# Attention probabilities of a Perceiver layer: half of each head transposed by DMA and DVE block transposes instead of TensorE

## The reference

```python
q = (query @ w_q).reshape(B, Q, HEADS, HEAD_DIM).transpose(0, 2, 1, 3)
k = (key @ w_k).reshape(B, Kl, HEADS, HEAD_DIM).transpose(0, 2, 1, 3)
v = (value @ w_v).reshape(B, Kl, HEADS, HEAD_DIM).transpose(0, 2, 1, 3)
scores = jnp.einsum('bhqd,bhkd->bhqk', q, k) * scale
attn = jax.nn.softmax(scores, axis=-1)
out = jnp.einsum('bhqk,bhkd->bhqd', attn, v)
return out.transpose(0, 2, 1, 3).reshape(B, Q, HEADS * HEAD_DIM) @ w_o
```

## Time and profile before

| | us |
|---|---|
| median of 3 runs | 644.96 (642.53 to 646.65) |
| profiled execution | 644.93 |
| its span | 643.0 |
| PE, DVE, ACT, POOL busy | 613.4, 461.1, 393.2, 263.8 |

### The profile page before, as it was taken

The page is one execution under the profiler, slowest core; times in us unless marked ns, Lnnn a source line. Parts: engine busy times, 40 slices in busy tenths (PEclk is TensorE's granted clock), DMA queues, the critical chain, the costliest instruction groups (busy, mean ns, idle before and its releaser), DMA issues.

```text
span 643.0 us, 11082 instructions
## 1 busy us (share of the span) xinstructions
PE 613.4 (95%) x4235; PEld 541.0 (84%) x4235; DVE 461.1 (72%) x816; ACT 393.2 (61%) x834; POOL 263.8 (41%) x252
## 2 busy tenths in 40 slices
PE   7899999999999999999999999999999999988797
PEld 4689899999998999978898989887999889875584
DVE  3666666778767687878776777878777777866863
ACT  4665566676665654877654965867565856742461
POOL 2210001131102104997344156997252347964533
PEclk9899999999999999999999999999999999998999
DMA  9910000020100004340030027140030008022923
GB/s 194 248 34 2 1 0 1 1 66 3 66 1 1 2 2 183 156 136 1 1 137 1 1 70 295 44 136 1 1 138 1 1 13 329 1 70 84 359 105 140
DMA packets 21403, 48.56 MB, mean 76 GB/s; under 512 B 1508, under 2 KB 14696, under 8 KB 17256
## 3 DMA queue, kind: packets, MB, share of 16 engines
q0 software_dynamic: 4608, 34.74, 14.4%
q1 hardware_dynamic: 16168, 12.85, 7.5%
q10 hardware_dynamic: 576, 0.26, 0.1%
HBM read 47.59 MB, written 0.26 MB: 74 GB/s over the span
## 4 chain that ended last, share of the span: by engine, by line
PE 65%; POOL 15%; DVE 7%; DMA 5%; ACT 4%; issue 3%; SPq 1%; POOLq 0%; DVEq 0%; ACTq 0%
PE ps_av L505 23%; PE ps_s L505 23%; PE ps_ring L780 13%; POOL leaf L1637 6%; PE ps_m L505 4%; POOL leaf L1641 2%; DMA leaf<-wk_t_dram 2%; DVE pt_lo L1231 2%; DMA prob<-down_q_dram,idx 2%; POOL ct_lo L1606 2%; POOL leaf L1678 1%; DVE chunk_max L1488 1%; ACT pt_hi L1073 1%; POOL leaf L1660 1%; ACT prob L1142 1%
## 5 line engine op out<-in xcount | busy, mean ns | idle before, releaser
L1073 ACT CAST pt_hi<-ps_ring 128x512 fp32r<-128x512 f32 x256 | 144.6, 590 | 145.2 <-PE ps_ring L780 145.1
L1231 DVE TENSOR_TENSOR pt_lo<-ps_ring,pt_hi 128x512 fp32r<-128x512 f32 x256 | 170.4, 686 | 57.2 <-ACT pt_hi L1073 55.2
L1142 ACT ACTIVATE prob<-ps_s,neg_max 128x1024 f32<-128x1024 f32 x128 | 141.6, 1113 | 25.9 <-DVE neg_max L1571 25.7
L505 PE MATMUL ps_av<-pt_hi,c_hi 128*128 128x256 f32 x512 | 150.3, 293 | 2.2 <-issue 1.6
L1488 DVE TENSOR_REDUCE chunk_max<-ps_s 128x1 f32<-128x1024 f32 x128 | 150.6, 1216 | 1.9 <-PE ps_s L505 1.9
L780 PE MATMUL ps_ring<-ident,prob 128*128 128x128 f32 x1024 | 145.0, 274 | 5.0 <-DVE pt_lo L1231 3.2
L505 PE MATMUL ps_av<-pt_lo,c_hi 128*128 128x256 f32 x512 | 144.7, 283 | 0.0
L505 PE MATMUL ps_av<-pt_hi,c_lo 128*128 128x256 f32 x512 | 144.6, 282 | 0.0
L780 PEld LDWEIGHTS ps_ring<-ident,prob 128*128 128x128 f32 x1024 | 121.4, 141 | 24.4 <-issue 6.0
L505 PE MATMUL ps_s<-ct_hi,q_hi 128*128 128x512 f32 x256 | 112.4, 439 | 4.8 <-POOL ct_lo L1606 2.9
L505 PE MATMUL ps_s<-ct_hi,q_lo 128*128 128x512 f32 x256 | 101.3, 396 | 0.0
...
## 6 DMA issues: line engine op xcount, KB each, us to landing
...
```

Source lines behind the costliest of these rows:

```text
L505: return nc.tensor.matmul(o, l, r, start=start, stop=stop)
L1073: nc.scalar.copy(pt_hi[:, pp, row:row + KPC, P * (n % 2):P * (n % 2 + 1)], ps_ring[:, i % 2, :].rearrange("p (k q) -> p k q", k=KPC)).then ...
L1142: nc.scalar.activation(prob[:, n % 2, 1024 * e:1024 * (e + 1)], ps_s[:, 1024 * e:1024 * (e + 1)], ACT.Exp, bias=neg_max[:, n:n + 1], accum ...
L1231: return nc.vector.tensor_tensor(o, a, b_, op)
```

## The change

For heads 4 to 61 the first half of the keys (0 to 1023) is no longer transposed by PE. The SP queue moves that half of `prob` in four DMAs of 128 rows of 1 KB, one for each group of 32 partitions, into the room of `pt_lo`: partition 32a+r gets the queries 4r to 4r+3 at the keys 256a to 256a+255. DVE then transposes 32x32 blocks, two instructions of 128x512 (`turn_blocks`), into a free room (`qmask` and `qk_ab`, or `leaf[0]`). Partition p then holds the keys 8p to 8p+7, so the context rows of the first half are loaded in that order. ACT casts both turned groups (`upper_moved`); the low part of the first is subtracted by POOL, of the second by DVE (`take_lower`). The second half of the keys still goes through PE and the ring, now before DVE's maximum, and is the first half of the context product. SP's queue now has the moves in it, with the context loads between them.

The diff, cut to its core:

```diff
+FIRST_MOVED, END_MOVED = 4, HEADS - 2
+
+
+def moved(head):
+
+    return FIRST_MOVED <= head < END_MOVED
+
+
+def groups_turned(head):
+
+    return (2, 3) if moved(head) else (2, 3, 0, 1)
+
+
+def moved_before(head):
+
+    return head - FIRST_MOVED
+
+
 def ring_items(slot):
 
     if slot >= HEADS:
         return DRAIN[slot - HEADS] if slot - HEADS < len(DRAIN) else []
 
-    out = [("T", slot - 2, g) for g in range(CH)] if slot >= 2 else []
+    out = [("T", slot - 2, g) for g in groups_turned(slot - 2)] if slot >= 2 else []
...
-        pt_hi = sb("pt_hi", [P, 3, KT // 2, 2 * P], F32R)
-        pt_lo = sb("pt_lo", [P, 3, KT // 2, 2 * P], F32R)
+        pt_hi = sb("pt_hi", [P, 3, 2, NK // 2], F32R)
+        pt_lo = sb("pt_lo", [P, 3, 2, NK // 2], F32R)
...
-            return (0, kt) if kt < KT // 2 else (1 + pair % 2, kt - KT // 2)
+            return (1 + pair % 2, kt) if kt < KT // 2 else (0, kt - KT // 2)
+
+        def moved_half(n):
+
+            return (slice(None), 1 + (n // 2) % 2, n % 2)
+
+        def moved_group(n, g):
+
+            return moved_half(n) + (slice(512 * g, 512 * (g + 1)),)
+
+        def has_moved(n):
+
+            return S[f"moved{n % 2}"], 64 * (moved_before(n) // 2 + 1)
+
+        def turned_room(n, g):
+
+            if n + 2 < H or (n + 2) % H >= 12:
+                return (qmask[:].rearrange("p h q -> p (h q)")[:, 512 * (n % 2):512 * (n % 2 + 1)],
+                        qk_ab[:].rearrange("p a b -> p (a b)"))[g]
+            o = 512 * (2 if g else n % 2)
+            return leaf[0][:, o:o + 512]
+
+        def split_place(c):
+
+            return (c + 2) % CH
+
+        def take_lower(eng, n, g):
+
+            o = moved_group(n, g)
+            return eng.tensor_tensor(pt_lo[o], turned_room(n, g), pt_hi[o].bitcast(F32), ALU.subtract)
...
+                if c < 2:
+                    rows = ctx_rows[b, 0:NK // 2, :].rearrange("(p j) d -> p j d", p=P)[:, KPC * c:KPC * (c + 1), :]
+                    sp.dma_start(by_key_tile(stage[:, c, :]), rows).then_inc(S[f"ld_st{c}"], 16)
+                    return
...
+            def move(n):
+
+                sp.wait_ge(S["exp_done"], 2 * n + 1)
+                if n // 2 >= 2:
+                    sp.wait_ge(S["av_done"], 2 * (n // 2 - 2) + 2)
+                if moved(n - 2):
+                    sp.wait_ge(S["blocks_turned"], 2 * moved_before(n - 2) + 2)
+                room = pt_lo[moved_half(n)].bitcast(F32).rearrange("p (s c) -> p s c", s=4)
+                for a in (0, 2, 1, 3):
+                    sp.dma_start(room[32 * a:32 * (a + 1)], prob[:, n % 2, 256 * a:256 * (a + 1)])\
+                        .then_inc(S[f"moved{n % 2}"], 16)
...
-            for b in range(B):
-                if b + 1 < B:
+            for n in range(HEADS):
+                if moved(n):
+                    move(n)
+                if n and n % H == 0:
                     for c in range(CH):
-                        load_ct(CH * (b + 1) + c)
+                        load_c(CH * (n // H) + c)
+                if n % H == 4 and n // H + 1 < B:
                     for c in range(CH):
-                        load_c(CH * (b + 1) + c)
-                if b >= 1:
-                    store(sp, b - 1)
+                        load_ct(CH * (n // H + 1) + c)
+                if n in (H * 3 - 3, H * 4 - 3):
+                    store(sp, n // H - 2)
...
-                    last = nc.tensor.transpose(o[:, i * P:(i + 1) * P], prob[:, n % 2, k:k + P], ident[:])
+                    rows = prob[:, n % 2, k:k + P]
+                    if g < 2:
+                        rows = prob[:, n % 2, 0:NK // 2].rearrange("p (k j) -> p j k", j=KT // 2)[:, KPC * g + i]
+                    last = nc.tensor.transpose(o[:, i * P:(i + 1) * P], rows, ident[:])
...
-                pe.wait_ge(S["ring_free"], BY_DVE[("T", 2 * pair + 1, 2 * half_no + 1)])
+                if half_no == 1 or not moved(2 * pair + 1):
+                    pe.wait_ge(S["ring_free"], BY_DVE[("T", 2 * pair + 1, 2 * half_no + 1)])
+                else:
+                    lower_parts(pair)
                 if pair % PPB == 0:
-                    pe.wait_ge(S["c_split"], CH * b + 2 * (half_no + 1))
-                if half_no == 0 and pair >= 1:
+                    pe.wait_ge(S["c_split"], CH * b + 2 * (2 - half_no))
+                if half_no == 1 and pair >= 1:
                     pe.wait_ge(S["av_taken"], pair)
-                elif half_no == 1 and 2 * pair + 3 in BESIDE:
+                elif half_no == 0 and 2 * pair + 3 in BESIDE:
                     pe.wait_ge(S["beside_free"], BESIDE[2 * pair + 3])
                 context_quarter(pair, 2 * half_no)
                 context_quarter(pair, 2 * half_no + 1).then_inc(S["av_done"], 1)
 
+            def lower_parts(pair):
+
+                pe.wait_ge(S["low_dve"], moved_before(2 * pair + 1) + 1)
+                pe.wait_ge(S["low_pool"], moved_before(2 * pair + 1) + 1)
...
-                    mm(ps_av[:, 0:2 * P], c_hi[:, kt, :], pt_hi[:, pp, row, :], first, False)
-                    mm(ps_av[:, 0:2 * P], c_hi[:, kt, :], pt_lo[:, pp, row, :], False, False)
-                    last = mm(ps_av[:, 0:2 * P], c_lo[:, kt, :], pt_hi[:, pp, row, :], False, end)
+                    first, end = kt == first_tile(pair), kt == last_tile(pair)
+                    o, at = ps_av[:, 0:2 * P].rearrange("p (j q) -> p j q", j=2), (slice(None), pp, slice(None), slice(P * row, P * (row + 1)))
+                    mm(o, c_hi[:, kt, :], pt_hi[at], first, False)
+                    mm(o, c_hi[:, kt, :], pt_lo[at], False, False)
+                    last = mm(o, c_lo[:, kt, :], pt_hi[at], False, end)
...
-                    transposes(tr, 2)
-                    transposes(tr, 3)
+                    for g in groups_turned(tr)[2:]:
+                        transposes(tr, g)
...
-                    context_half((s - 3) // 2, 0)
+                    context_half((s - 3) // 2, 1)
                 if s % 2 == 0 and 4 <= s < HEADS:
-                    context_half((s - 4) // 2, 1)
+                    context_half((s - 4) // 2, 0)
...
+            def upper_moved(n, g):
+
+                act.wait_ge(S["blocks_turned"], 2 * moved_before(n) + g + 1)
+                nc.scalar.copy(pt_hi[moved_group(n, g)], turned_room(n, g)).then_inc(S["upper_moved"], 1)
...
+                        act.wait_ge(*has_moved(n - 2))
...
-                    if 2 <= s < HEADS:
-                        upper_pt(s - 2, g)
+                    if 2 <= s < HEADS and not moved(s - 2):
+                        upper_pt(s - 2, groups_turned(s - 2)[g])
+                    elif 2 <= s < HEADS and g < 2:
+                        upper_pt(s - 2, 2 + g)
+                    if moved(s - 2) and g in (0, 2):
+                        upper_moved(s - 2, g // 2)
...
+            def turn_blocks(n):
+
+                dve.wait_ge(*has_moved(n))
+                if moved(n - 2):
+                    dve.wait_ge(S["low_pool"], moved_before(n - 2) + 1)
+                rows = pt_lo[moved_half(n)].bitcast(F32).rearrange("p (s k j) -> p s j k", s=4, j=KT // 2)
+                for g in range(2):
+                    if g and moved(n - 1):
+                        dve.wait_ge(S["low_dve"], moved_before(n - 1) + 1)
+                    nc.vector.transpose(turned_room(n, g).rearrange("p (j r s) -> p s j r", j=KPC, s=4),
+                                        rows[:, :, KPC * g:KPC * (g + 1), :]).then_inc(S["blocks_turned"], 1)
+
+            def lower_moved(n, g):
+
+                dve.wait_ge(S["upper_moved"], 2 * moved_before(n) + g + 1)
+                take_lower(nc.vector, n, g).then_inc(S["low_dve"], 1)
...
+                if s < HEADS and moved(s - 2):
+                    turn_blocks(s - 2)
...
-                    lower(tr, 0)
-                    lower(tr, 1)
+                    lower(tr, 2)
+                    lower(tr, 3)
...
-                    lower(tr, 2)
-                    lower(tr, 3)
+                    if moved(tr):
+                        lower_moved(tr, 1)
+                    else:
+                        lower(tr, 0)
+                        lower(tr, 1)
...
+                    pool.wait_ge(S["low_pool"], moved_before(H * b + 25) + 1)
+                    pool.wait_ge(S["low_dve"], moved_before(H * b + 25) + 1)
...
+                    pool.wait_ge(S["upper_moved"], 2 * moved_before(s - 2) + 1)
+                    pool.wait_ge(S["blocks_turned"], 2 * moved_before(s - 2) + 2)
+                    take_lower(nc.gpsimd, s - 2, 0).then_inc(S["low_pool"], 1)
```

More of the change, by code:

```diff
@@ L799, in context_quarter @@
                     pp, row = part(pair, kt)
-                    first, end = kt == 0, kt == KT - 1
-                    mm(ps_av[:, 0:2 * P], c_hi[:, kt, :], pt_hi[:, pp, row, :], first, False)
-                    mm(ps_av[:, 0:2 * P], c_hi[:, kt, :], pt_lo[:, pp, row, :], False, False)
-                    last = mm(ps_av[:, 0:2 * P], c_lo[:, kt, :], pt_hi[:, pp, row, :], False, end)
```

(11 more changed lines are left out.)

32 lines of the change are left out of this document (17 added, 15 removed).

## The result

The change made the kernel slower: 701.79 us (median of 4 runs, 701.73 to 702.21) against 644.37 of the kernel before beside it (642.53 to 646.65), a ratio of 1.089 with a 95% interval of 1.085 to 1.093. The profiled execution took 702.21 us, span 700.4, 57.3 us over that of before.

The account below looks back on a forecast made before the run. PE bounded the kernel before; afterwards a loop through ACT and DVE would mostly take its place. Terms -4.4 - 2.3 - 6 - 10 + 7 + 0 + 4 = -11.7 from 644.93 us gave 633 us, range 614 to 664.

Parts of the forecast that it names:

- what the transposes give: Eight of sixteen PE transposes go for 58 heads: 0.87 us each, 50 us at most, only where PE stays the bound.
- either rival's price: DVE's block transpose: 0.69 us, one element after the other (624 us, chance 0.22), or 1.41, strided both sides (662, 0.14).
- The three stretches up to slot 28: From 55.1 to 248.9 us: -4.4 for five slots, -2.3 for eight, -6 for ten.
- the plain slot: Work of one head, 7.83 us before: forecast 7.65 us, between the loop's mean 7.5 and longer slot 7.8.
- a loop through ACT: Exponentials, ACT's casts, subtraction, DVE's maxima, back to exponentials: 7.2 us, 7.8 every second slot, mean 7.5, taking PE's place.
- the sign that the forecast named: In plain slots, ACT's exponentials wait less for DVE's last reduction than DVE waits for ACT's second cast; no size given.
- the moves behind the gathers: SP queue while leaf rows are gathered: moves take 12 us, some 4 late; a third counted three times, +4 us.
- moves late: Rival: the gathers hold up all moves, 633 + 8 = 641 us; chance 0.06.
- POOL's queue: From 248.9 to 301.5 us and twin: two or three POOL subtractions ahead of each DVE or PE wait, +3.5 us each.
- the stretches 301.5 to 389.6 and its twin: Ten slots each, PE 78.0 and DVE 79.8 us of work, taken as 83 us: -5 us each.
- the locked port: Rival: DVE's subtraction with two SBUF operands waits for POOL's running instruction, 21 us in all, 654 us; chance 0.22.
- its own split: Chances of the cases: forecast 0.36, one element 0.22, locked port 0.22, both sides strided 0.14, late moves 0.06.

Follow-up runs that it names:

- k2: The changed kernel with the moves of heads 28, 29, 44, 45, 60 and 61 halved to two parts of 128 KB each; 685.34 us.
- a: The changed kernel with head pairs 28/29, 44/45 and 60/61 not moved, all four of their groups kept on TensorE; 663.6 us.
- e2: Kernel a with POOL subtracting the turned group ahead of the folds, not behind them, in slots 17, 33 and 49; 648.2 us.
- b: The changed kernel with DVE's two-operand subtraction of the second turned group replaced by a one-operand row maximum, result incomplete; 687.45 us.
- i: Kernel g with DVE's subtraction of a turned group replaced by a one-operand row maximum, result incomplete; 628.4 us.
- g: The changed kernel with heads 28 to 33, 44 to 49, 60 and 61 not moved, kept on TensorE; 635.98 us.
- d: The changed kernel with the edits of a, b and c together, result incomplete; 633.86 us.
- c: The changed kernel with POOL's subtraction of the first turned group and its place in POOL's queue left out, result incomplete; 668.95 us.

## Why the prediction was wrong

The forecast was 633.0 us in a range of 614 to 664, and the time came out above the range. Its steps, one by one:

**Right in size: what the transposes give, and the price of a turn.** The 1.05 us taken for the block transpose, the price of the strided reduction in the earlier trace rows, was measured as 1.17 to 1.19 us of duration and 1.07 from start to start, nearer to it than to either rival's price. The three stretches up to slot 28 were forecast at -12.7 us in all and gave -12.1.

**Right in the number only: the plain slot.** 7.65 us were forecast and 7.57 measured (60.54 / 8), but the forecast had them from a loop through ACT, in which DVE waits for ACT's second cast and PE has gaps. From 95.75 to 156.29 us DVE waits 0.6 us in all for ACT's casts from the ring, ACT's exponentials wait 20.4 us for DVE's last reduction, the opposite of the sign that the forecast named, and PE is busy for 59.76 of 60.54 us. DVE's own work fills the slot: 58.81 / 8 = 7.35 us. The forecast had that load at 7.3 and did not take it for the bound; that loop and load lie so close together is luck.

**Failed first: the moves behind the gathers, +4 us (bounds 0 and 12).** The mechanism, packets that take turns, was right in part; the size was off by six to ten times. The forecast had 32 packets at 0.37 us, 12 us to the landing, some 4 us late, and counted a third of that lateness three times. Measured were 0.42 us a turn (3.9 us for 150 pairs on 16 engines), near the forecast, but 8.8 us to the first part's landing and 20.1 from the first issue to the last landing, of which turns explain a part; DVE stood idle for 9.0 us. And the whole wait counts, because all the work that ends the slot stands behind the turn in DVE's program: 259.20 to 265.44. The idle time on moves is 24.1 us, six times the term and twice its upper bound. Half the bytes in these moves gave 16 us back (k2), no moves, turns and subtractions of these heads 38 (a). The rival "moves late" had 8 us more, 641.

**Failed second: POOL's queue, +3.5 in each of two stretches and 0 in the last.** The forecast counted how long POOL's subtractions take ahead of a wait (two or three times 1.29 us). What counted is where they stand: head 31's is behind folds that wait 3.04 us for ACT and take 5.8 themselves, and PE's context product waits for it. Measured by order alone (a to e2): 15 us, and the wait lies in slots 35 and 51, which the forecast had in the stretches 301.5 to 389.6 and its twin, at -5 each with POOL off the path.

**Failed third: the locked port, left to a rival at 0.22.** The row that spoke for it, the 128x16 operation of 1.24 us in the earlier trace rows, was read rightly and not used in the sum. For the subtraction it is so: 4.30 us beside the 4.61 us product, 0.68 without; mean 1.22 to 1.27. The Trainium skill (SBUF — State Buffer, Who interferes with whom) has the rule that two SBUF inputs on DVE and a reading GpSimd instruction exclude each other, and a reduction does not; b and i bear out both halves. The row itself is of an operation with one SBUF operand, which these two kernels don't explain: it took 1.23 to 1.24 us three times before, 0.17 in the change and 3.26 in i. Its price in the rival, 21 us, was near enough: 14.3 us in b, 7.6 between g and i. But alone it would have given 654, still far from 702.

The stretches 301.5 to 389.6 were thus to gain 5 us and, slot 35 aside, gained nothing: with the one-operand operation slots 36 to 45 gain 4.0 (b), so the slow subtraction took that back.

Sum of the measured pieces: -12 for the plain slots, +38 for the moves, +15 for POOL's order, +14 for the slow subtraction make 55 of the 57 us. This is an account and not a proof of each: the pieces overlap, as d shows, a's 38 holds more than the moves, and POOL's whole part would be 33 by c. Shown is that the three together give 68 us back (d). The forecast gave each of the three a place, two of them as small terms and one as a rival by itself; that they come together, mostly in the same six slots of an entry (30 to 35), was not in any of its cases.

The forecast's chances also don't follow from its own split: by that, "same" comes to 0.19 and "slower" to 0.35, where it gave 0.25 and 0.29.
